# Attention layer of a graph network: ScalarE's step begins with the exponential of the softmax, ahead of the copies of turned h rows

## What is computed

```
h = relu(layernorm(x))
q, k, v = h@Wq+bq, h@Wk+bk, h@Wv+bv
alpha = sum(q[dst] * k[src]) / sqrt(32)            # per head
ea    = exp(alpha - segment_max(alpha, dst)[dst])
alpha = ea / (segment_sum(ea, dst)[dst] + 1e-16)
x = x + segment_sum(v[src] * alpha, dst) + h@Wskip + bskip
h = relu(layernorm(x))
... second layer: x = x + h_self + segment_sum(in_degree * (h[src] + edge features @ We), dst)
```

## Time and profile before

| | us |
|---|---|
| median of 3 runs | 1672.98 |
| lowest and highest | 1672.11, 1676.85 |
| the profiled execution, its own time | 1668.93 |
| its span, first to last instruction | 1667.2 |

### The profile page before, as it was taken

How to read it: one execution, slowest core, us unless ns; L and a number is a source line. 1 busy time by engine, 2 the same in 40 slices (tenths; PEclk the granted TensorE clock), 3 DMA queues, 4 the chain that set the end, 5 groups by cost and what they waited for, 6 DMA issues and landing times. The chain is left out here.

```text
span 1667.2 us, 34575 instructions
## 1 busy us (share of the span) xinstructions
PE 1465.7 (88%) x10645; PEld 1264.1 (76%) x10646; DVE 1303.2 (78%) x3599; ACT 1061.4 (64%) x2601; POOL 1074.7 (64%) x1208
## 2 busy tenths in 40 slices
PE   5889888698999999999999984899999899989998
PEld 4667766588888888888888883777777677777776
DVE  8889765188989888898989885677777677776776
ACT  5878888665666666666666641665665665656664
POOL 2565442577777666666766623777777777777774
PEclk9999999899999999999999996999999999999999
DMA  8889898556666656666566625577676677676673
GB/s 218 277 272 305 280 310 262 166 150 181 183 185 178 181 174 178 176 176 180 170 184 168 185 61 139 135 167 168 158 172 160 151 166 168 159 171 152 163 169 95
DMA packets 164789, 303.82 MB, mean 182 GB/s; under 512 B 105752, under 2 KB 109940, under 8 KB 159761
## 3 DMA queue, kind: packets, MB, share of 16 engines
q1 hardware_dynamic: 123740, 202.16, 42.6%
q0 software_dynamic: 40896, 99.90, 23.7%
HBM read 197.23 MB, written 104.50 MB: 181 GB/s over the span
## 5 line engine op out<-in xcount | busy, mean ns | idle before, releaser
L882 POOL DMA_INDIRECT sb_kv<-kv_rows,sb_src_all x500 | 473.5, 947 | 217.2 <-issue 112.4
L910 POOL DMA_INDIRECT sb_kv<-x_rows,sb_src_all x500 | 473.9, 948 | 205.3 <-issue 109.5
L1827 ACT ACTIVATE sb_hn<-sb_xn 100x128 f32<-100x128 f32 x500 | 240.6, 481 | 263.0 <-DMA sb_kv<-x_rows,sb_src_all 229.2
L1830 ACT ACTIVATE sb_vw<-sb_kv 128x128 f32<-128x128 f32 x500 | 239.7, 479 | 0.0
L1739 ACT ACTIVATE sb_hn<-sb_xn,sb_nstat 100x128 f32<-100x128 f32 x500 | 229.5, 490 | 0.0
L1914 PE MATMUL ps_b<-sb_w,sb_memberT 128*125 128x256 f32 x800 | 201.8, 392 | 22.1 <-DVE sb_xn L1000 12.6
L1501 DVE COPY sb_hT<-ps_b 128x400 f32<-128x400 f32 x250 | 142.4, 570 | 94.5 <-PE ps_b L2143 93.1
L1914 PEld LDWEIGHTS ps_b<-sb_w,sb_memberT 128*125 128x125 f32 x800 | 147.6, 194 | 44.3 <-issue 16.2
L2143 PE MATMUL ps_b<-sb_member,sb_vw 128*128 128x100 f32 x1000 | 173.9, 278 | 0.0
L1761 ACT ACTIVATE sb_memberT<-ps_b 100x512 f32<-100x512 f32 x150 | 77.7, 518 | 146.2 <-PE ps_b L2009 146.2
L2143 PEld LDWEIGHTS ps_b<-sb_member,sb_vw 128*128 128x128 f32 x1000 | 157.2, 198 | 9.8 <-issue 9.8
(11 more groups left out here) (202 smaller groups left out, 3113.9 us busy)
## 6 DMA issues: line engine op xcount, KB each, us to landing
kv_rows<-sb_kv SPq DMA_DIRECT2D x26, 1120.0 KB
sb_xn<-x_rows SPq DMA_DIRECT2D x50, 507.8 KB
sb_xn<-in_x SPq DMA_DIRECT2D x50, 500.0 KB
out_rows<-sb_xo SPq DMA_DIRECT2D x49, 500.0 KB
x_rows<-sb_xo SPq DMA_DIRECT2D x24, 1015.6 KB
sb_kv<-in_edge_attr SPq DMA_DIRECT2D x500, 32.0 KB
sb_kv<-in_x SPq DMA_DIRECT2D x28, 560.0 KB
kv_rows<-sb_xn SPq DMA_DIRECT2D x13, 1120.0 KB
```

The lines of the kernel that those rows point to most:

```text
L882: pool.indirect_dma_start(out=kvs[:, k % 4, t, :], out_offset=None, in_=kv_rows, in_offset=bass.IndirectOffsetOnAxis(ap=src_all[:, n:n + 1 ...
L910: pool.indirect_dma_start(out=xs1[:, k % 4, t, :], out_offset=None, in_=x1, in_offset=bass.IndirectOffsetOnAxis(ap=src_all[:, n:n + 1], ax ...
L1827: nc.scalar.activation(hn1[:, t, :], xn1[:, k % 4, t, 0:D], ACT.Relu, scale=xn1[:, k % 4, t, D:D + 1], bias=xn1[:, k % 4, t, D + 1:XW]).th ...
L1830: nc.scalar.activation(hs1[:, t, :], xs1[:, k % 4, t, 0:D], ACT.Relu, scale=xs1[:, k % 4, t, D:D + 1], bias=xs1[:, k % 4, t, D + 1:XW]).th ...
```

## The change

ACT's `step0(k)` issues the exponential of batch k-1 as its first instruction. Before, it stood behind the two copies of turned h rows of batch k+1 and the first `relu` of batch k+2. Nothing else differs; the instructions are the same.

```diff
             def step0(k):
                 nxt = real(k + 1)
+                if real(k - 1):
+                    exps(k - 1)
                 if nxt:
                     copy_h(k + 1, 0)
                     copy_h(k + 1, 1)
                 relus(k + 2, 0, 1)
-                if real(k - 1):
-                    exps(k - 1)
                 if nxt:
                     copy_q(k + 1, 0)
```

## The result

| | before | after |
|---|---|---|
| median, us | 1672.55 | 1630.43 |
| lowest and highest | 1670.54, 1676.85 | 1625.58, 1631.48 |
| the profiled execution, its own time | 1668.93 | 1631.48 |
| its span | 1667.2 | 1629.7 |

The ratio is 0.9739, with a 95% interval of 0.9712 to 0.9766: the change makes the kernel 42 us faster. Forecast were 35 us and 1638.1, in a range from 1631 to 1654. So the side, the place and the mechanism came out as forecast, and the gain was larger than I had computed, just past the end of the range.

What follows compares the result with a forecast made beforehand. A loop through ACT's queue, with the exponential behind the copies, was taken as the bound. Gains of 35.4 us, less 1.0 in step 4, plus 0.5 at the start, gave 34.9: from 1672.98 to 1638.1 us, range 1631 to 1654.

Steps and rivals of the forecast that it cites:

- What bounds the kernel: Attention layer's steady steps: PE and DVE wait for one another through the loop; DVE waits 55.1 us, PE 41.9 us.
- the loop: PE turns weights, then next h rows; ACT copies those, then does the exponential; DVE makes weights for PE; 13.64 us.
- The mechanism in even steps: Exponential runs in ACT's idle time before the copies; PE no longer waits for weights, gaining 0.96 us a step.
- The term of the odd step: Copies start 0.36 us late but weights come earlier; a gain of 0.67 us in each of 22 odd steps.
- The cost in step 4: Gathered rows come late there, so copies queue behind the exponential; cost 0.9 to 1.0 us, taken as 1.0.
- Step 48: The last step with copies; PE waits only 0.49 us there, so the gain is 0.5 us.
- the start: Steps 1 to 3, where gathers pace the layer: a gain between 0 and 1.6 us, taken as 0.5.
- Odd steps gain nothing: Copies late by more than 0.36 us eat the odd steps' gain; 20.2 us gained, 1652.8 us; chance 12%.
- No change: Another path of 13.64 us closes the loop, so the time stays the same; chance 5%.
- Slower by stretched gathers: Denser DVE stretches gathers past 1.364 us, POOL paces the layer; at 1.40 us 16 us slower, 1689; chance 4%.
- More than forecast: Both kinds of step save all of the wait, 38.5 us, and 1.6 from the start: 1633 us; chance 7%.

Runs made afterwards that it cites:

- experiment 2: Against the changed kernel, the exponential stands behind both copies of h rows but ahead of the one Relu; 1651.62 us, ratio 0.9882 to the kernel before.
- 4: Against the changed kernel, the exponential moved behind the first copy of q, one place later than in the kernel before; 1749.64 us, ratio 1.0469 to before.
- 10: The kernel before with two (first kernel) or four (second) more exponentials into a spare tile ahead of the real one; 1680.55 and 1701.66 us, ratios 1.0055 and 1.0193.
- experiment 5: The changed kernel with the exponential done twice a step, first into a tile nobody reads; 1630.02 us, ratio 0.9754 to the kernel before.
- experiment 3: Against the changed kernel, the exponential stands between the two copies of h rows in all steps; 1628.41 us, ratio 0.9750 to the kernel before.
- experiment 6: Against the changed kernel, the exponential is first in even steps from 6 on, between the copies elsewhere; 1623.01 us, ratio 0.9714 to the kernel before.
- 9: The changed kernel with the order of experiment 6 plus PE's second membership product ahead of the third skip projection; 1621.24 us, ratio 0.9712 to before.
- experiment 8: The changed kernel with nine gathers a batch in place of ten from batch 4 on; 1621.73 us, ratio 0.9702 to the kernel before.
- 7: The changed kernel with PE's second membership product of the next batch moved ahead of the third skip projection; 1623.76 us, ratio 0.9715 to before.

## Where the prediction was right, and the step that failed

**What bounds the kernel: right.** The exponential's place in ACT's queue set the loop. Half of the move gives about half of the gain (experiment 2), a move in the other direction costs (4), and added exponentials lengthen each step by their own length (10).

**The mechanism in even steps: right, the term slightly small.** "PE then no longer waits": shown. The term was 0.96 and measured 1.06. The prediction put PE's turn at 0.42 us after the start of the last membership products, from 0.39 us of their row plus 0.03; the rows of after have 0.31, for the products' row and the next one overlap on PE.

**The term of the odd step: the step that failed.** It said 0.67 "between 0.57 (the PE row) and 0.77 (all of DVE's wait)"; it measured 0.99, with the mechanism as described. (Its own sum for the PE row gives 0.59 and not 0.57.) Three things were mis-sized in it, all in one direction:
- *The copies are less late.* I had them "0.36 late", from the exponential's row length plus two gaps of 0.04 and 0.02. On ACT one row's end lies over the next one's start: experiment 5 shows 0.22 us for an exponential whose row is 0.31 (789.18 and 789.40). PE's membership products began 5.44 us into the step, 0.20 later than before and not 0.36.
The Trainium skill, "ScalarE: Activation LUTs", section "What ACT_TABLE_LOAD costs", says that back-to-back ACTIVATEs overlap by about 93 ns; the trace agrees, with 0.09 us here.
- *PE turns the weights 0.32 us after those products began*, as in even steps: together 0.85 instead of 0.59.
- *DVE's idle time was no upper bound.* "0.77 (all of DVE's wait)" counts from the end of the row ahead, and DVE's rows overlap as well: after, a statistics row of 0.18 starts 0.10 us before the scan does. The scan starts 3.19 us into the step (800.49) and not 4.03 (802.59 - 798.56), 0.84 earlier. And from the scan to the weighing it is 2.86 us in place of 3.03, of which 0.11 is the shorter `tot_e`. Together 1.01. The forecast had no term for `tot_e`: nothing in its argument would have shortened it, so this 0.11 us came as luck.

By steps, 22 x 0.99 + 21 x 1.06 = 44.0; the rows of steps 5 to 47 give 42.96, since steps 5 to 14 of before were a little shorter than later ones. Forecast were 34.9. These 8.1 us account for the miss: 1638.1 - 8.1 = 1630.0, and 1630.43 was measured.

**The cost in step 4: right.** Forecast +1.0, measured +0.84 at an equal clock (0.75 and 0.76 over the step). The rows of after show how it is paid:

```profile
378.94 0.69 DVE L1298 TENSOR_TENSOR sb_prod<-ps_b,sb_kv 128x512 f32<-128x512 f32 x1 [5.60 <-DMA sb_kv<-kv_rows,sb_src_all]
...
380.75 0.31 ACT L1780 ACTIVATE sb_er<-sb_dl 40x128 f32<-40x128 f32 x1 [6.21 <-DVE sb_dl L1328]
...
381.57 0.67 PE L1989 MATMUL ps_b<-sb_bsplit,sb_ones_b 128*100 128x512 bf16 x1 [0.77 <-ACT sb_hT L1746]
```

The gathers come late, `dl` too, the copies stand behind it, and PE waits 0.77 us for them. Its projection starts 2.63 us into the step (381.57 - 378.94), where in before it was 1.82 (378.42 - 376.60), 0.81 later. With the exponential between the copies step 4 takes 13.66 us in experiment 3, at a clock of 0.75; the 12.39 and 12.33 of experiments 6 and 9 are at 0.86. Step 48 was right within 0.1 us and the start within 0.3.

**The rivals.** *Odd steps gain nothing* fell: they gained 0.99 us, nearly as much as even ones. The danger behind it is real but small, since experiment 5 shows that what stands ahead of the copies costs one for one there. *No change* fell with the step lengths. *Slower by stretched gathers* fell: a gather averages 0.956 us where it had 0.946, and experiment 8 shows that a POOL with only the 0.30 us between its gathers isn't what the step waits for. *More than forecast* had the right sign and too low a ceiling: it took 0.77 and 0.98 as all that there was. My range ended at 1631 because I took the idle time in a row for the most that could be gained; a row's idle time leaves out the overlap with the row ahead, and the work behind it can become shorter too.

**What stays open.** Why the gathers of batch 4 are late in some kernels and not in others (experiments 8 and 10), and why the clock falls behind some waits of 2.02 us and not behind others (4). That `tot_e` sets the odd steps of experiments 7 and 9 is read from the lengths of steps; no run changes `tot_e` alone.

## What to carry to other kernels

Where two engines are each near 90% and both wait once a step, look for a small instruction that stands behind larger, unrelated ones in a third engine's queue: that queue joins two chains to one loop, and taking it out is worth what stood ahead of it, until the next longest way round. Measure what an instruction costs its queue from start to start, not by the length of its row: here 0.22 us and not 0.31. Such overlaps, with one DVE operation that became 0.11 us shorter, made a term of 0.99 us look like 0.67. When the exact place matters, try it by kind of step: here step 4, whose data come late, and the odd steps did better with the first copy ahead of the exponential, and the even steps with the exponential first. And look at the granted clock of a stretch before its length is put down to an edit.

## What the runs showed of the hardware

**The phase between a gather and a DVE operation.** I had expected the gathers to be stretched evenly or not at all. Instead one DVE operation and one gather meet at the same phase each step. `tot_e` (L1335) takes 0.33 us where it starts 0.65 to 0.67 us into a gather, in 29 of 30 steps of before between 500 and 900 us; the gather then takes its usual 0.94. In odd steps of after it starts 0.34 to 0.38 us into one and takes 0.22, and that gather takes 1.07 to 1.10, as in the rows at 801.01 and 801.38 above (500 to 900 us, as for all phases here). In the first kernel of experiment 10 it starts mostly 0.50 or 1.05 us in and both are short. Where `tot_e` is stretched by a gather that is under way, its end stays put: in before and in experiments 2, 6, 7 and 9 it starts 0.52 to 0.72 us into the gather and ends 0.99 to 1.03 us after the gather's start, so it takes 0.47 us from 0.52, 0.42 from 0.57 and 0.33 from 0.66. Where the gather is stretched, it ends 0.72 to 0.73 us after `tot_e` starts: it is 0.99 us long with a start at 0.27, 1.08 with 0.35 and 1.12 with 0.40 (experiment 2, after, experiment 4). So a small move of phase is worth 0.11 us a step or more on DVE's chain. It went the right way in experiments 2 and 3, in after's odd steps and in experiment 10, and the wrong way in the odd steps of 7 and 9. In the even steps of experiment 6 `tot_e` takes 0.40 to 0.42 us mostly and costs nothing (12.590), since DVE waits for PE there.
The Trainium skill, "SBUF — State Buffer", section "SBUF: two separate sides", describes the ports that VectorE and GpSimd share as an exclusive lock that goes to whoever starts first, while the other blocks. The rows fit that one of the two is delayed and not both, but no run here shows that it is this lock. The delay is 0.11 us for `tot_e` in before and 0.13 to 0.16 for the gather in after, not a whole gather of 0.94.

**The granted clock and short waits.** A wait of PE of 0.98 us (before) and 1.27 us once a step leaves the granted clock at 1.00, and so does 1.67 us in the steady part. Behind 1.77 and 1.90 us it fell to 0.50 once each, and behind another wait of 1.77 us, in step 4 of the same kernel, it didn't. In experiment 4, with 2.02 us in each step, it fell in about every second step, 16 of 31. So the length of one wait doesn't decide it alone, and the runs don't show what does. Each fall cost 1.7 us of step, nearly as much as the wait itself.
